# Self-attention: scores in pairs, the values of a step in two halves of 256 queries

## The reference

```python
# layer 0: cross-attention to the context, with a residual
Q, K, V = x @ Wq + bq, ctx @ Wk + bk, ctx @ Wv + bv
x = softmax(Qh @ Kh.T / 4) @ Vh + x                  # per head
# layer 1
q, k, v = split(layernorm(x) @ sa_in_w.T + sa_in_b)
x = x + merge(softmax(qh @ kh.T / 4) @ vh) @ sa_out_w.T + sa_out_b   # self-attention
x = x + merge(attention(layernorm(x), ctx)) @ co_w.T + co_b          # cross-attention
x = x + gelu(layernorm(x) @ w1.T + b1) @ w2.T + b2
```

## Time and profile before

| | us |
|---|---|
| median of 3 runs (896.5 to 901.94) | 898.55 |
| the profiled execution | 903.44 |
| its span | 901.7 |
| PE busy in the span | 762.8 (85%) |
| DVE busy | 518.5 (57%) |
| ACT busy | 418.9 (46%) |
| POOL busy | 119.3 (13%) |

### The profile page before, as it was taken

One profiled execution on the slowest core, in us unless ns is written; L12 is line 12 of the kernel. 1 busy time (PEld: TensorE's weight loads), 2 busy tenths in 40 slices (PEclk: granted clock), 3 DMA queues, 4 the chain that ended last, 5 costly groups with the idle time before them and its releaser, 6 DMA issues.

```text
span 901.7 us, 10733 instructions
## 1 busy us (share of the span) xinstructions
PE 762.8 (85%) x3824; PEld 379.2 (42%) x3824; DVE 518.5 (57%) x805; ACT 418.9 (46%) x770; POOL 119.3 (13%) x241
## 2 busy tenths in 40 slices
PE   6328778748899999999899998897987788899998
PEld 3124434423533333333343333332443445457667
DVE  1225475369688888888888888861364456340001
ACT  2105434212177777777666665655543344522120
POOL 9501014030000000000000100102021001230000
PEclk9758879969799999999999999998799789999999
DMA  7765432544731304040404010124062630000001
GB/s 244 203 209 129 102 98 70 190 94 166 182 97 19 55 3 72 2 73 1 73 1 73 2 22 2 36 72 108 3 166 73 145 76 3 2 0 24 18 12 41
DMA packets 37557, 66.82 MB, mean 74 GB/s; under 512 B 6848, under 2 KB 17216, under 8 KB 37504
## 3 DMA queue, kind: packets, MB, share of 16 engines
q1 hardware_dynamic: 37216, 66.05, 29.2%
q10 hardware_dynamic: 288, 0.08, 0.0%
HBM read 36.33 MB, written 28.22 MB: 72 GB/s over the span
## 4 chain that ended last, share of the span: by engine, by line
PE 64%; DVE 15%; SPq 7%; DMA 6%; ACT 3%; POOL 2%; issue 2%; DVEq 0%; POOLq 0%; ACTq 0%
PE PV L725 16%; PE ST L711 15%; DVE nm L928 8%; PE SM L656 6%; PE ST L619 5%; PE ST L615 5%; SPq L476 4%; DMA stacks<-mrow 4%; PE SM L596 3%; PE SM L606 2%; PE SM L676 2%; PE SM L663 2%; POOL stacks L1024 2%; PE PV L619 2%; PE PV L615 2%
## 5 line engine op out<-in xcount | busy, mean ns | idle before, releaser
L824 ACT ACTIVATE prob<-ST 128x512 f32<-128x512 f32 (+1 forms) x640 | 337.5, 600 | 244.2 <-PE ST L711 244.0
L928 DVE TENSOR_REDUCE nm<-SM 128x2 f32<-128x1024 f32 x256 | 303.7, 1220 | 65.9 <-PE SM L656 63.9
L725 PE MATMUL PV<-prob,Vst 128*32 128x512 f32 x1280 | 181.0, 639 | 4.1 <-ACT pvT L813 3.2
L711 PE MATMUL ST<-stacks 64*128 64x512 f32 x512 | 177.2, 474 | 8.3 <-DMA stacks<-mrow 4.0
L656 PE MATMUL SM<-stacks 64*128 64x512 f32 x512 | 115.8, 436 | 33.9 <-DVE nm L928 20.8
L711 PEld LDWEIGHTS ST<-stacks 64*128 64x128 f32 x512 | 72.0, 187 | 161.3 <-ACT prob L824 138.7
L931 DVE TENSOR_REDUCE nm<-SM 128x8 f32<-128x624 f32 x64 | 51.5, 805 | 64.0 <-PE SM L663 62.6
L656 PEld LDWEIGHTS SM<-stacks 64*128 64x128 f32 x512 | 55.6, 189 | 61.0 <-DVE nm L928 42.9
L711 PE MATMUL ST<-stacks,Kc 128*77 128x512 f32 x128 | 53.5, 500 | 32.7 <-DMA stacks<-mrow 31.0
L1094 POOL CAST mp<-na 128x16 fp32r<-128x16 f32 x48 | 9.6, 199 | 447.9 <-DVE na L963 284.3
L663 PE MATMUL SM<-Kc,stacks 128*128 128x156 f32 x256 | 49.8, 327 | 15.9 <-DMA stacks<-q_rows 13.9
(11 more groups left out here) (98 smaller groups left out, 674.5 us busy)
## 6 DMA issues: line engine op xcount, KB each, us to landing
q_rows<-split SPq DMA_DIRECT2D x72, 256.0 KB
stacks<-q_rows SPq DMA_DIRECT2D x48, 384.0 KB
k_rows<-split SPq DMA_DIRECT2D x24, 256.0 KB
stacks<-k_rows SPq DMA_DIRECT2D x16, 384.0 KB
stacks<-mrow SPq DMA_DIRECT2D x192, 4.0 KB
fm<-in_xT SPq DMA_DIRECT2D x4, 512.0 KB, 9.1
X<-in_x SPq DMA_DIRECT2D x4, 512.0 KB, 3.5
V<-in_w SPq DMA_DIRECT2D x2, 1024.0 KB, 10.0
```

The source lines that it names most:

```text
L711: mm(ST[0:att.keys, n % 3, :], keys_of(att, g, h, kt), QST[att.name][g % att.buffers][rows, h // 2, j * BLK:(j + 1) * BLK], start=True, st ...
L725: last = mm(PV[h * 32:(h + 1) * 32, :], Vst[:, g % 2, kt, h, :], prob[:, t % 2, h, :], start=(kt == 0), stop=(kt == att.kt - 1))
L824: act_fn(prob[0:att.keys, t % 2, h, :], ST[0:att.keys, n % 3, :], ACT.Exp, scale=SCALE) \
L928: ins = vec.tensor_reduce(nm[:, q % 2, c, tile, 2 * n:2 * n + 2], ps.rearrange("p (s k) -> p s k", s=2), AX.X, ALU.max, negate=True)
```

## The change

In A1 the scores no longer run three ahead. A step issues scores 0 and 1 of its own, the first slots' side work, and the first half (256 queries) of the values of the step before; then scores 2 and 3, the last slots' side work, and the second half of those values. `values` gets the first query and the count; it waits for the exponentials at the first half only, starts the sum in the bank with the first half of tile 0, and signals at the second half. Each half loads the same weights. ACT's copy of PV stands behind the fourth exponential. A0 and A2 call `values` with all 512 queries at the place where they did before.

```diff
@@ TensorE
-                def values(t):
+                def values(t, first, count):
...
-                    if kt == 0:
+                    if kt == 0 and first == 0:
                         pe.wait_ge(vst_ready, att.g0 + g + 1)
                         if att.q0 + q >= 1:
                             pe.wait_ge(pv_out, att.q0 + q)
-                    pe.wait_ge(exp_done, (att.t0 + t + 1) * QUAD)
+                    if first == 0:
+                        pe.wait_ge(exp_done, (att.t0 + t + 1) * QUAD)
+                    queries = slice(first, first + count)
                     for h in range(QUAD):
-                        last = mm(PV[h * 32:(h + 1) * 32, :], Vst[:, g % 2, kt, h, :], prob[:, t % 2, h, :],
-                                  start=(kt == 0), stop=(kt == att.kt - 1))
-                    last.then_inc(pv_done, 1)
+                        last = mm(PV[h * 32:(h + 1) * 32, queries], Vst[:, g % 2, kt, h, :], prob[:, t % 2, h, queries],
+                                  start=(kt == 0 and first == 0), stop=(kt == att.kt - 1 and first + count == BLK))
+                    if first + count == BLK:
+                        last.then_inc(pv_done, 1)
...
-                if att.whole:
-                    score_units(0, 3)
                 for t in range(att.last):
                     work = att.side(t)
-                    if att.whole and 1 <= t <= att.steps:
-                        values(t - 1)
                     for n in range(PAIR):
-                        if att.whole:
-                            score_units(t * QUAD + 3 + 2 * n, 2 - n)
-                        else:
-                            score_units(t * QUAD + 2 * n, 2)
-                            if n == 1 and 1 <= t <= att.steps:
-                                values(t - 1)
+                        for h in range(2 * n, 2 * n + 2) if t < att.steps else []:
+                            scores(t, h)
+                        if not att.whole and n == 1 and 1 <= t <= att.steps:
+                            values(t - 1, 0, BLK)
                         for slot, w in work:
                             if slot // 2 == n:
                                 side(att, w)
-                    if att.whole:
-                        score_units(t * QUAD + 6, 1)
+                        if att.whole and 1 <= t <= att.steps:
+                            values(t - 1, n * BLK // 2, BLK // 2)
@@ ScalarE
-                            if att.whole and h == 2 and q is not None:
-                                values_out(att, q)
-                        if pair == 1 and q is not None and (not att.whole or t >= att.steps):
+                        if pair == 1 and q is not None:
                             values_out(att, q)
```

More of the change, by code:

```diff
@@ L722, in values @@
                             pe.wait_ge(pv_out, att.q0 + q)
-                    pe.wait_ge(exp_done, (att.t0 + t + 1) * QUAD)
+                    if first == 0:
+                        pe.wait_ge(exp_done, (att.t0 + t + 1) * QUAD)
+                    queries = slice(first, first + count)
                     for h in range(QUAD):
-                        last = mm(PV[h * 32:(h + 1) * 32, :], Vst[:, g % 2, kt, h, :], prob[:, t % 2, h, :],
-                                  start=(kt == 0), stop=(kt == att.kt - 1))
-                    last.then_inc(pv_done, 1)
+                        last = mm(PV[h * 32:(h + 1) * 32, queries], Vst[:, g % 2, kt, h, :], prob[:, t % 2, h, queries],
+                                  start=(kt == 0 and first == 0), stop=(kt == att.kt - 1 and first + count == BLK))
+                    if first + count == BLK:
+                        last.then_inc(pv_done, 1)
                 ring_empty(att)
                 pe.wait_ge(pad_ready, 2)
-                def score_units(first, count):
-                    for n in range(first, min(first + count, att.steps * QUAD)):
-                        scores(*divmod(n, QUAD))
-                if att.whole:
-                    score_units(0, 3)
                 for t in range(att.last):
                     work = att.side(t)
-                    if att.whole and 1 <= t <= att.steps:
-                        values(t - 1)
                     for n in range(PAIR):
-                        if att.whole:
-                            score_units(t * QUAD + 3 + 2 * n, 2 - n)
-                        else:
-                            score_units(t * QUAD + 2 * n, 2)
-                            if n == 1 and 1 <= t <= att.steps:
-                                values(t - 1)
+                        for h in range(2 * n, 2 * n + 2) if t < att.steps else []:
+                            scores(t, h)
+                        if not att.whole and n == 1 and 1 <= t <= att.steps:
+                            values(t - 1, 0, BLK)
                         for slot, w in work:
```

## The result

| us | before | after |
|---|---|---|
| median | 900.25 (4 runs, 896.5 to 903.99) | 868.57 (4 runs, 864.69 to 873.17) |
| the profiled execution, its span | 903.44, 901.7 | 873.17, 871.4 |

The ratio is 0.9641 (0.9604 to 0.9678): 3.6% faster, against a forecast of 870. In the runs made for the last experiments the same kernel stood at 869.96, ratio 0.965 (0.9615 to 0.9686).

The account below looks back on a forecast made before the run. Plain self-attention steps were taken as bound by the loop score, exponential, score, values (2.60 us). 19.5 (first 64 steps) + 9.4 (later steps) = 28.9 off the profiled 903.44 gives 874.5; off the median, 870; range 855 to 898.

Parts of the forecast that it names:

- (1): Plain steps of self-attention: score pairs each followed by a maximum and half of the values; 2.60 to 2.44 us, -0.16.
- Rival D: A half of values costs less (0.50), exponentials bind plain steps at 2.36; 6 us more won, 863; chance 0.06.
- (2): Step with the maxima's transpose: half of the values goes in front of the wait; 3.71 to 3.05 us, -0.66.
- (3): Step with the block's transposes, PV's copy later: 4.07 to 3.34 us, -0.73; block 21.03, first 64 steps win 19.5.
- (4): The other 56 self-attention steps up to 621.31 us, with projections and transposes of the next block: 9.4 us won.
- an extra product and the block's transposes: Six late self-attention steps with both: wait for PV's copy isn't covered, -0.25 us each by estimate, -1.5 in all.
- (5): Stop until 626.78 us: PE's 4.29 us wait for rows of maxima doesn't shrink, takes back up to 1 us.
- B: Fixed cost per pass or VectorE eats the plain steps' gain, only long steps win 14 us: 885; chance 0.14.
- C: A half of values doesn't shrink as its columns do: 909 at 0.80 us a half, 948 at 1.00; chance 0.10.
- E: Gain given back at the change to the next attention, where PE waits for DMA anyway: 896; chance 0.08.

Follow-up runs that it names:

- quarters: Changed kernel with each half of the values as two calls of 128 queries in a row; 874.09 us, ratio 0.9683.

## Why the prediction was right

The mechanism is the one it gave: the loop from score to exponential to score to values was shortened by halving the values and standing one half behind each pair, until it was no longer than PE's own order. The two kernels with one part each show that neither part shortens the loop in the place where it was tried alone. By its steps:

(1) A half of values was taken at 0.57 (bounds 0.43 and 1.00) and measured 0.57. Plain steps came to 2.47 against 2.44: score to values is 0.66, not 0.655, and a half from its load 0.57. Eight passes of 256 columns lost exactly the streaming of the other 256. The Trainium skill ("TensorEngine Tiling (Array Packing)", Instruction Overhead) says that each matmul has about 60 cycles of overhead, which by an estimate from that page would have made the step 2.64; the trace doesn't agree for passes in four column tiles, as twice the passes took the same 1.00 and the same 0.57 above.

What failed in this step is its floor: "the loop can't go under 2 x 1.18 = 2.36". A step without any maximum took 2.24:

```profile
581.56 0.19 PEld L711 LDWEIGHTS ST<-stacks 64*128 64x128 f32 x2 [0.41 <-ACT prob L816]
581.99 0.16 PEld L727 LDWEIGHTS PV<-prob,Vst 128*32 128x32 f32 x8 [0.25 <-ACT prob L816]
582.15 2.07 ACT L816 ACTIVATE prob<-ST 128x512 f32<-128x512 f32 x4 [0.22 <-PE ST L711]
582.56 0.43 PEld L711 LDWEIGHTS ST<-stacks 64*128 64x128 f32 x2 [0.41 <-issue]
...
583.23 0.16 PEld L727 LDWEIGHTS PV<-prob,Vst 128*32 128x32 f32 x8 [0.24 <-issue]
...
583.80 0.19 PEld L711 LDWEIGHTS ST<-stacks 64*128 64x128 f32 x2 [0.41 <-ACT prob L816]
```

The prediction let an exponential hold up each pair. Here only the fourth score is held: the loads of its pair take 0.43 instead of 0.19, and the values follow 0.67 behind the pair instead of 0.43. So the loop passes the exponential once in a step: 0.59 from the first score to its exponential, 0.65 to the fourth score, 0.43 to the values, 0.57 to the next step's first score, 2.24 as measured. The 0.59 is a second miss in this step: the prediction took 0.53, which gave the exponentials 0.04 of room. In plain steps it is 0.59 as well (326.18 to 326.77), and why it isn't 0.53 is open. With maxima the loop is 0.59 + 0.65 + 0.66 + 0.57 = 2.47, and PE's own order is 2 x (0.66 + 0.57) = 2.46: the two meet in the plain step, and no run tells which of them sets it. Rival D's bound of 2.36 isn't there.

(2) Predicted 3.05, measured 3.05, with the second maximum's matmul 2.05 behind the step's first scores (318.20 to 320.25) against 2.06. The run with half the maximum shows how much of it is that wait: the step kept 2.93, so the first maximum costs it 0.12, and the rest above a plain step is PE's own order with one more piece in it.

(3) Predicted 3.34, measured 3.35; the copy of PV 2.73 behind the start of the step before (328.65 to 331.38), as said, and values 0.30 late against 0.29. The whole block was given as 21.03 and is 21.21 to 21.24: six plain steps at 0.03 more.

That is also most of what the first 64 steps lack: 17.25 won instead of 19.5. Eight blocks at 0.2 are 1.6; the rest lies in the first block, which has no block before it to transpose and so nothing to win in that step. From its first score to the next block's it went from 22.34 to 21.56, and won 0.78.

(4) The late steps won 12.88 instead of 9.4. They are 54 and not 56; the two too many stand among those priced at nothing. Steps with extra transposes alone came from 3.71 to 3.79 down to 3.25 (predicted 3.22). The six with a piece of output projection stayed at 23.02 and 23.20 together (predicted: no change). Those with both a projection and the block's transposes went from 4.54 to 4.77 (-0.23 each, predicted -0.25). Three terms were mis-sized. Half of the steps counted as "an extra product and the block's transposes" carry extra transposes in place of the product (81, 97, 105): priced at a loss of 0.25 each, they won 1.6 together. Step 98, priced at nothing, won 0.9. And three of the steps without maxima won 0.37 each instead of 0.16.

But 1.55 us of this the change can't claim. In the profiled execution before, the granted clock fell for a while in steps 97 and 98:

```profile
545.00:552.00 7.00, 6.47 (x31) 2.40 (x31) 4.42 (x7) 2.48 (x5) 0.00 (x0) 0.76 0.00 0
```

They took 6.34 and 3.39 there. In the run of halves without pairs, whose other late steps agree with those of before within 0.02, the clock stood at 1.00 and they took 5.57 and 2.61. So the change itself won about 11.3 in this stretch.

(5) The stop stayed, as forecast, but by another cause. The wait for rows fell to 0.8 us, in which PE still had values to stream, and that for the next attention's stack took its place at 3.7: since scores no longer run ahead, the first maximum of the next attention now stands in front of the last block's first scores, and not behind them (the waits, 584 to 600 us):

```profile
PE SM L663 <- DMA stacks<-q_rows: 3.7, 1, 3.7
...
PEld ST L711 <- DMA stacks<-mrow: 0.8, 1, 0.8
```

That the steps behind it come out even can't be judged: steps 120 to 126 took 29.15 us before, and 31.44 and 26.27 in two executions of the changed kernel.

The sum was right partly by luck, because two errors cancel: -2.3 in the early steps, +3.5 in the late ones, of which 1.55 is the clock in one execution. One reading was weak as well: the 130.4 us of the earlier trace rows were taken for waits of PE. Part of that time PE streams values, as the row of after shows, where 82.8 us remain though plain steps have no such wait.

Of the rivals, B and C are refuted by the measured half, and B's other reason, VectorE, by the run with half the maximum. E isn't seen: what follows step 118 differs by less than 0.3 us in all, though that too is two differences that cancel. Steps 119 to 127 lost 2.2 us, and what follows won 2.5; that last part takes from 237.1 to 241.4 us in the profiled executions of all kernels here, so a difference of 2.5 in it says little.

## What to carry to other kernels

Where an engine's order loops through another engine (score, exponential, free bank, score), look at what stands in each part of the loop: work cut in two and put evenly into its gaps can hide what neither the cut nor the new order hid alone here. Read a bound from a step in which the suspected engine has nothing to do, and test it by taking that engine's work away: VectorE, busy 96% of a block, set neither the plain step nor the one with the block's transposes, and half of its work taken away gave 0.12 in the one with the maxima's transpose. A wait that is moved without its cause goes to the next one in line; follow the chain until the thing that is waited for can itself be needed later.

## What the runs showed of the hardware that was not expected

Matmuls in four column tiles cost by their columns, whatever the number of passes: 8 passes of 512 and 16 of 256 in 1.00 us, 8 of 256 and 16 of 128 in 0.57. Against the streams of the earlier trace rows a fixed 0.14 us is left in both (1.00 - 2 x 0.429, 0.57 - 2 x 0.216). It comes once for each group of values that stands between scores, and not once a pass: two halves in a row pay it once, two halves apart twice.

A stop of some microseconds cost twice in these runs, once itself and once by the clock behind it. In the profiled execution with quarters PE stopped once for 2.56 us with no wait that the profile shows (PE, then the window of the stop and the one behind it):

```profile
297.76 0.43 PE L727 MATMUL PV<-prob,Vst 128*32 128x128 f32 x8 [2.56 <-issue]
```

```profile
296.00:300.30 4.30, 2.54 (x30) 1.33 (x30) 1.34 (x2) 1.08 (x2) 0.00 (x0) 0.82 0.01 1
300.30:309.10 8.80, 8.80 (x103) 4.61 (x103) 5.87 (x6) 5.28 (x10) 0.00 (x0) 0.70 0.02 6
```

The mean granted clock was 0.82 in the first and 0.70 in the second window, and the two steps after the stop took 4.54 and 3.74 instead of 3.05 and 2.47, with a half of values marked 1.08 instead of 0.64: of the 5.5 us that this block lost (26.79 against 21.24), about half is the stop and half the clock. Ahead of it, loads of the stacks kept the DMA engines 0.83 busy (291 to 296 us); whether instructions came late for that reason is open, as no run tried it.
